# Running the first matmuls (P1) of the next product ahead of the last ones (P4) of the current product, in a fused convolution and pooled-attention kernel

## What is computed

```python
qk  = relu(bn(conv1x1(x, qk_w)))            # 256 channels
val = relu(bn(conv1x1(x, v_w)))             # 512 channels
key, value = psp(qk), psp(val).T            # max over 1x1, 3x3, 6x6 and 8x8 grids: 110 cells
scores = softmax(query @ key * 256 ** -0.5) # query is qk, 4096 positions
y = scores @ value
return x + bn(conv1x1(y, out_w))
```

## Time and profile before

| | |
|---|---|
| median of 3 runs | 1330.21 us (1327.58 to 1331.76) |
| the profiled execution's own time | 1328.02 us |
| its span, first to last instruction | 1326.2 us |
| busy: TensorE / VectorE / GpSimd / ScalarE | 97% / 72% / 72% / 52% |
| matmuls | 5539 |
| granted TensorE clock, mean | 0.998 |
| the chain that ended last | TensorE 73%, VectorE 10%, GpSimd 6%, ScalarE 6%, issue 3%, DMA 1% |

### The profile page before, as it was taken

One profiled execution on the slowest core, in us unless ns is written; L12 is line 12 of the kernel. 1 busy time (PEld: TensorE's weight loads), 2 busy tenths in 40 slices (PEclk: granted clock), 3 DMA queues, 4 the chain that ended last, 5 costly groups with the idle time before them and its releaser, 6 DMA issues.

```text
span 1326.2 us, 16789 instructions
## 1 busy us (share of the span) xinstructions
PE 1284.6 (97%) x5539; PEld 1035.4 (78%) x5539; DVE 957.4 (72%) x2171; ACT 688.2 (52%) x1017; POOL 952.3 (72%) x414
## 2 busy tenths in 40 slices
PE   7999999999999999999999999999999998999996
PEld 6777788887888778887788877888788876888874
DVE  6455677778777778778777777777877776876566
ACT  4333555654555654455654455664455546654421
POOL 2888988876887867887777787887788734755622
PEclk9999999999999999999999999999999999999999
DMA  6323356666676646667556666656657668986226
GB/s 223 111 96 112 111 186 210 205 205 213 205 238 232 209 163 224 224 222 236 179 199 232 228 209 217 212 195 218 223 199 243 216 218 314 315 301 225 95 96 254
DMA packets 134537, 272.20 MB, mean 205 GB/s; under 512 B 9226, under 2 KB 9266, under 8 KB 134450
## 3 DMA queue, kind: packets, MB, share of 16 engines
q1 hardware_dynamic: 133874, 270.07, 60.3%
q10 hardware_dynamic: 576, 1.05, 0.2%
HBM read 174.61 MB, written 96.47 MB: 204 GB/s over the span
## 4 chain that ended last, share of the span: by engine, by line
PE 73%; DVE 10%; POOL 6%; ACT 6%; issue 3%; DMA 1%; SPq 0%; DVEq 0%; ACTq 0%; POOLq 0%
PE conv_ps L687 15%; PE conv_ps L689 15%; PE conv_ps L691 15%; POOL xl L578 5%; PE out_ps L773 3%; PE out_ps L774 3%; PE out_ps L775 3%; PE conv_ps L672 3%; PE conv_ps L673 3%; PE conv_ps L671 3%; DVE row_max L1319 2%; PE score_ps L744 2%; PE score_ps L745 2%; ACT xh L958 2%; PE score_ps L743 2%
## 5 line engine op out<-in xcount | busy, mean ns | idle before, releaser
L1319 DVE TENSOR_REDUCE row_max<-conv_ps 128x64 f32<-128x384 f32 (+2 forms) x576 | 283.7, 529 | 149.0 <-ACT q_out L1029 68.2
L578 POOL TENSOR_TENSOR xl<-xa,xh 128x1024 fp32r<-128x1024 f32 x108 | 257.7, 2409 | 87.0 <-ACT xh L958 87.0
L687 PE MATMUL conv_ps<-xh,sh 128*128 128x512 f32 x648 | 254.3, 392 | 8.8 <-DVE conv_ps L1382 3.1
L689 PE MATMUL conv_ps<-xh,sl 128*128 128x512 f32 x648 | 254.4, 393 | 0.0
L691 PE MATMUL conv_ps<-xl,sh 128*128 128x512 f32 x648 | 254.3, 392 | 0.0
L578 POOL TENSOR_TENSOR xl<-tt,xh 128x1024 fp32r<-128x1024 f32 x81 | 194.2, 2411 | 15.6 <-ACT xh L958 15.6
L687 PE MATMUL conv_ps<-xh,wh 128*128 128x512 f32 x486 | 189.5, 390 | 2.7 <-POOL xl L578 2.7
L691 PE MATMUL conv_ps<-xl,wh 128*128 128x512 f32 x486 | 190.8, 392 | 0.0
L689 PE MATMUL conv_ps<-xh,wl 128*128 128x512 f32 x486 | 190.7, 392 | 0.0
L966 ACT ACTIVATE conv_ps<-conv_ps 128x512 f32<-128x512 f32 x81 | 47.2, 583 | 260.4 <-PE conv_ps L691 249.5
L1459 DVE SCALAR_TENSOR_TENSOR xo<-out_ps,shift,xo 128x512 f32<-128x512 f32 x205 | 151.9, 745 | 30.5 <-PE out_ps L775 17.5
(11 more groups left out here) (227 smaller groups left out, 2537.5 us busy)
## 6 DMA issues: line engine op xcount, KB each, us to landing
xa<-x SPq DMA_DIRECT2D x148, 512.0 KB, 5.4
xo<-x SPq DMA_DIRECT2D x104, 512.0 KB, 4.2
out<-xo SPq DMA_DIRECT2D x104, 512.0 KB, 3.5
queries<-q_out SPq DMA_DIRECT2D x112, 256.0 KB, 2.3
q_in<-queries SPq DMA_DIRECT2D x50, 512.0 KB, 4.1
tt<-x SPq DMA_DIRECT2D x13, 512.0 KB, 5.2
out<-tt SPq DMA_DIRECT2D x13, 512.0 KB, 3.8
early<-queries SPq DMA_DIRECT2D x6, 512.0 KB, 7.1
```

Of the source, the lines that this page charges most:

```text
L578: nc.gpsimd.tensor_tensor(xl[:, b0:b1, :], raw, xh[:, b0:b1, :], ALU.subtract).then_inc(x_lo, 1)
L687: nc.tensor.matmul(out[:, :], hi[:, k, :], xh[:, b + k, :], start=first, stop=False, skip_group_check=True)
L689: nc.tensor.matmul(out[:, :], lo[:, k, :], xh[:, b + k, :], start=False, stop=False, skip_group_check=True)
L1319: last = nc.vector.tensor_reduce(row_max[:, c, n, :], src[:, r0_ * W:r1_ * W].rearrange("p (r w) -> p w r", w=W), AX.X, ALU.max)
```

## The change

The part P1 leaves the head of `pair_product` and becomes a function of its own, `first_product`. It is called for the very first product at its old place, and for every other product between fill3 and P4 of the product before. The waits of P1 go with it. Nothing else is changed: the same matmuls, the same waits, no order on another engine.

```diff
+            def first_product(s, j):
+                n = product(s, j)
+                m1 = slice(HALVES[j][0] * P, (HALVES[j][0] + 1) * P)
+                if j == 0:
+                    pe.wait_ge(x_lo, part_number(s, 0))
+                pe.wait_ge(rows_pooled, pair_group(s, j) - 3)
+                out = pair_banks(n)[0]
+                for k in range(HALF):
+                    nc.tensor.matmul(out[:, :], wh[:, k, m1], xh[:, k, :], start=(k == 0), stop=False,
+                                     skip_group_check=True)
+                    nc.tensor.matmul(out[:, :], wl[:, k, m1], xh[:, k, :], start=False, stop=False,
+                                     skip_group_check=True)
+                    last = nc.tensor.matmul(out[:, :], wh[:, k, m1], xl[:, k, :], start=False, stop=False,
+                                            skip_group_check=True)
+                last.then_inc(p1_done, 1)
+
             def pair_product(s, j, fill1, fill2, fill3, fill4):
...
-                x_ready(0)
-                pe.wait_ge(rows_pooled, g - 3)
-                times(u1, wh[:, K1, m1], wl[:, K1, m1], 0, start=True).then_inc(p1_done, 1)
+                if n == 0:
+                    first_product(1, 0)
                 fill1()
...
                 fill3()
 
+                if j < 2:
+                    first_product(s, j + 1)
+                elif s < PAIRS - 1:
+                    first_product(s + 1, 0)
+
                 x_ready(6)
                 pe.wait_ge(u7_made, n + 1)
```

## The result

| | before | after |
|---|---|---|
| median | 1329.95 us (1327.58 to 1334.95) | 1346.38 us (1344.7 to 1349.82) |
| runs | 6 | 6 |
| profiled execution / span | 1328.02 / 1326.2 us | 1345.73 / 1343.9 us |
| mean granted clock in it | 0.998 | 0.992 |

The ratio is 1.0125 (95% interval 1.0101 to 1.0149): 1.2% slower, 16.4 us, where 10.5 us were forecast. The time lies just outside the range of 1333 to 1346. The matmuls are the same 5539, so the loss is in the distances between their starts. The two profiled executions are 17.7 us apart. In the kernel after, the lines of VectorE, ScalarE and GpSimd have a number 20 higher (make_u4's addition is L1402, the copy of u1 L986), and the three matmuls of a part are L704, L706 and L708.

The account below looks back on a forecast made before the run. TensorE's matmuls plus pauses were taken to bound the pair stage. Five image pairs at 1.37 + 0.3 us (8.4) and 2.1 us for early pairs made 10.5 us: 1340.7 us, 0.8% slower, range 1333 to 1346.

Parts of the forecast that it names:

- The bound and the direction: Pair stage: TensorE's matmuls plus pauses set the time; only pauses, 7.4 us, can be won; slower had 0.81.
- Part 5 of an image pair: Five image pairs: u4 comes late behind P4, TensorE's pause grows from 0.65 to 2.0 us; 1.37 us each.
- Project (B0, 2): Same five image pairs: this projection waits for VectorE's late addition; 0.3 us each, bounds 0 and 0.8.
- The copy of u1: Turns of pairs: no cost at 20 ordinary ones; a pause of 1.2 instead of 0.3 us at three early ones.
- more slower: Rival, chance 0.14: the u1 copy misses its margin by 0.3 us at 20 ordinary turns, 6 us more, 1346.7.
- Pair 1 with GpSimd in the way: Pair 1: the weights' low parts wait for P4 and GpSimd; part 2 at 76.6 instead of 73.86, 2.7 us late.
- Pairs 1 to 4: Early pairs: late weights and pauses at turns, less covered waits for GpSimd; 2.1 us net, bounds 0.4 and 3.5.
- The clock: Rival, chance 0.05: the clock falls after the 2.0 us pauses; eight slow matmuls, 1.6 us, in five pairs, 1348.7.
- the second: The earlier trace's pause of 2.11 us, followed by matmuls at full speed.
- No change: Rival, chance 0.13: later pauses of the image pair make good the late u4, some 1 us each; 1334 or less.
- faster: Rival, chance 0.06: VectorE's chain does not hang on the relu or has slack; only the earlier P1 counts, 1325.

Follow-up runs that it names:

- e2: The changed kernel with P1 ahead only at turns from one pair to the next, its old place elsewhere; 1342.53 us, 1.0082 to the kernel before.
- e3: The changed kernel with u4 made ahead of refine on VectorE in the image pairs; 1337.3 us, 1.0048 to the kernel before.
- e5: The changed kernel with unneeded matmuls in the long pauses of pair 1 and five image pairs, waits kept; 1341.24 us, 1.0077 to the kernel before.
- e10: The changed kernel with the weights' low parts ahead of the fourth row maximum in pair 1; 1339.15 us, 1.006 to the kernel before.
- e9: The changed kernel with P1 ahead only inside pairs, u4 before refine, weights before the row maximum, projection (B0, 2) behind scores; 1319.77 us, 0.9916 to before.
- e12: The kernel before, P1 unmoved, with u4 before refine, weights before the row maximum, projection (B0, 2) behind scores; 1325.79 us, 0.9958 to before.
- e6: The changed kernel with P1 at its old place behind all three products of pair 1; 1340.29 us, 1.0064 to the kernel before.

## Why the prediction was wrong where it was, and right elsewhere

- **The bound and the direction: right.** TensorE sets the pair stage, the change could win few pauses, and it made longer ones. Slower had 0.81.
- **Part 5 of an image pair: right.** 1.37 forecast, 1.31 measured, five times; shown by e2 (there with the turns alone) and e3 (gone with u4 earlier).
- **Project (B0, 2): right, a little small.** 0.3 forecast, 0.39 measured and a share of slower first matmuls; the five image pairs made 9.5 instead of 8.4 us.
- **The copy of u1: right at both kinds of turn.** No pause at the 20 ordinary ones; 1.16 us in place of 0.3 at three early ones, forecast 1.2. The rival *more slower* is out: its 20 waits are not there.
- **Pair 1 with GpSimd in the way: the mechanism right, the figure with luck.** Part 2 at 76.89, forecast 76.6; both low parts ended 1.08 us behind GpSimd. Pairs 1 to 4 gave 1.3 us instead of 2.1, within the bounds. The start that the forecast went by, a pause of 1.66 us idle, lies between 0.82 and 2.55 in other executions with the same order, so the loss of pair 1 differs by as much. The sum of all waits, 10.8 by the profile and 10 to 12 by e5, was forecast at 10.5. The Trainium skill, "SBUF — State Buffer", section "SBUF: two separate sides", says that an operation of GpSimd and one of VectorE with two SBUF inputs exclude each other; these rows agree, and e10 showed it from the other side too, with GpSimd's operation at 3.38 us.
- **The clock: this step failed.** The rival said "My pause of 2.0 us (1.85 idle) is just below the second", and so gave the clock 0.05. It took one execution of one pause for a border. The pause that it went by is followed by the 1.2 GHz level in half of the profiles, and my own of 1.79 us in 10 of 25. In place of a clock that stays up, the change had a mean clock of 0.9905 against 0.994 over its executions, and 6.4 us of slow matmuls more in its profile. The size that the rival gave to a fall (eight matmuls, 1.6 us) was right; it happened in two of the five image pairs, not in all or none. An expected 0.4 x 5 x 1.55 = 3.1 us was missing from the sum.
- **The same step left pair 1 out.** My working moved part 2 of (1, 2) by 2.7 us from a pause of 1.66 idle, which makes an idle time of about 4 us, and the earlier trace rows have a row for just that: 4.41 idle, then 0.66 of the clock. The rival looked at the image pairs alone. That cost 2.4 us in the profile. With both, the sum were 10.5 + 3.1 + 2.4 = 16.0 us. That this is near the 16.4 measured is in part luck: the frequencies were counted afterwards, and the mean clocks of all executions and e5 put the clock at 4 to 6 us.
- **The Trainium skill**, "TensorE: Matmul & The Clock Gate", section "Part 1: The HAM clock gate", had been cited for the clock that halves after idleness, with the remark that the rows bore it out for the long pause alone. e5 showed it for the short ones: with the wait left as it was and TensorE kept at work, no matmul of the pair stage was slow.
- **No change and faster: out.** Nothing caught up. The gain of the earlier P1 is there, as e9 against e12 shows (6.0 us), and was below the loss.

What stays open: why the medians of e6 and e10 lie 8 us and more below the change when their profiles lie 2.7 and 5.4 below (the mean clocks point to falls elsewhere), and what decides whether a pause of 1.8 to 2.1 us lowers the clock.

## What to carry to other kernels

Moving work ahead on the engine that sets the time makes everything it passes late by its own length: list who waits for the postponed part before counting what the moved one wins, and move only where no chain hangs on it, or shorten that chain first (e9). Price a pause of TensorE with the clock in it, as a chance times the slow matmuls that may follow, from several executions and not from one row. Busy time hides the slow stretches; the distance between matmul starts and the granted clock show them.

## What was not expected of the hardware

- The same pause of 1.79 us idle was followed by seven or eight matmuls at 0.43 us in 10 of 25 cases and by full speed in the others, within one execution too (310.01 and 631.36 yes; 471.49, 792.82 and 952.69 no).
- Seven unneeded matmuls in a pause made the kernel faster: 1.0077 against 1.0125.
- A small VectorE operation of 128x440 elements took 0.61 us alone and up to 2.65 us in these rows: it ended 0.47 us behind the GpSimd operation of 2.4 us during which it began, in 83 cases of 84.
